# Attention orders on VectorE, key blocks turned two at a time, and the seam from a Mamba layer to a 2:4-sparse feed-forward

## What is computed

```
x = x + attention(layernorm(x))     # 16 heads of 128, clip, ALiBi, causal
x = x + ternary_ffn(layernorm(x))   # bf16, weights quantised by groups of 64
x = x + mamba(layernorm(x))         # 512 channels, 16 states, conv of 4
x = x + sparse_ffn(layernorm(x))    # h = silu(x Wg) * (x Wu), keep the 2 largest of each 4
```

```
scores = clip(q k^T / sqrt(128), -1024, 1024) + slope[h] * j, -inf where j > i
z = softmax(scores) v ;  out = z Wo
h_t = exp(delta_t A) h_(t-1) + delta_t B_t u_t ;  y_t = C_t h_t + D u_t ;  out = (y * silu(z)) Wout
```

## Time and profile before

| | us |
|---|---|
| median of 3 runs (1805.96 to 1808.68) | 1806.5 |
| the profiled execution | 1806.8 |
| its span, first to last instruction | 1804.9 |
| PE busy | 1667.8 (92%) |
| DVE busy | 1414.8 (78%) |
| ACT busy | 1272.2 (70%) |
| POOL busy | 824.5 (46%) |

### The profile page before, as it was taken

One profiled execution on the slowest core, in us unless ns is written; L12 is line 12 of the kernel. 1 busy time (PEld: TensorE's weight loads), 2 busy tenths in 40 slices (PEclk: granted clock), 3 DMA queues, 4 the chain that ended last, 5 costly groups with the idle time before them and its releaser, 6 DMA issues.

```text
span 1804.9 us, 31648 instructions
## 1 busy us (share of the span) xinstructions
PE 1667.8 (92%) x9536; PEld 1363.9 (76%) x9536; DVE 1414.8 (78%) x2299; ACT 1272.2 (70%) x2376; POOL 824.5 (46%) x731
## 2 busy tenths in 40 slices
PE   6899999999999999999997998789799799897998
PEld 4788888888888888888886787566467565456887
DVE  6688777877787777777776666888888788886996
ACT  4677767776777677777774554899895999783442
POOL 3555455545555455545542111059692088780000
PEclk9999999999999999999999999989999999998999
DMA  2000000000000000000001000022220122240000
GB/s 95 19 24 24 23 20 21 23 23 29 9 21 24 26 15 15 26 23 15 15 6 40 10 0 1 4 96 102 82 93 1 50 90 97 70 140 1 1 24 24
DMA packets 25090, 64.14 MB, mean 36 GB/s; under 512 B 2816, under 2 KB 8960, under 8 KB 24768
## 3 DMA queue, kind: packets, MB, share of 16 engines
q1 hardware_dynamic: 25024, 63.31, 10.6%
HBM read 60.94 MB, written 2.36 MB: 35 GB/s over the span
## 4 chain that ended last, share of the span: by engine, by line
PE 54%; POOL 15%; DVE 13%; issue 11%; ACT 5%; DMA 2%; POOLq 0%; DVEq 0%; SPq 0%; ACTq 0%
POOL m_h L2246 12%; PE ps L475 9%; PE ps L548 8%; PE ps L510 8%; PE ps L533 5%; PE ps L488 5%; PE ps L740 4%; PE ps L660 3%; POOL prob L2132 2%; PE ps L752 2%; PE ps L874 2%; PE ps L561 2%; PE ps L681 2%; DVE x L1520 2%; PE ps L908 1%
## 5 line engine op out<-in xcount | busy, mean ns | idle before, releaser
L2246 POOL TENSOR_TENSOR m_h<-m_h,m_C 128x1024 f32<-128x1024 f32 x128 | 305.8, 2392 | 193.9 <-DVE m_h L2024 193.9
L2024 DVE TENSOR_TENSOR_SCAN m_h<-m_y,ps 128x1024 f32<-128x1024 f32 x128 | 291.6, 2284 | 53.4 <-PE ps L867 45.9
L2132 POOL TENSOR_SCALAR prob<-prob 128x896 f32<-128x896 f32 (+7 forms) x256 | 195.8, 765 | 298.8 <-ACT prob L995 270.0
L2139 POOL TENSOR_SCALAR prob<-prob,rinv 128x128 f32<-128x128 f32 (+7 forms) x256 | 237.0, 929 | 161.7 <-DVE rinv L1508 152.3
L1481 DVE TENSOR_TENSOR pt_lo<-ps,pt_hi 128x512 fp32r<-128x512 f32 (+2 forms) x320 | 193.9, 606 | 96.0 <-ACT pt_hi L1008 92.3
L874 PE MATMUL ps<-m_h,ident 128*128 128x512 f32 x512 | 249.1, 610 | 10.8 <-POOL m_h L2246 10.8
L1474 DVE CUSTOM_DVE_ANT_0 prob<-prob,bias 128x640 f32<-128x640 f32 (+7 forms) x256 | 216.5, 859 | 46.8 <-POOL prob L2132 31.4
L1001 ACT ACTIVATE prob<-prob,nmax 128x128 f32<-128x128 f32 (+7 forms) x256 | 197.2, 773 | 43.6 <-DVE nmax L1474 43.6
L1008 ACT ACTIVATE pt_hi<-ps 128x512 fp32r<-128x512 f32 (+2 forms) x320 | 170.3, 532 | 76.3 <-PE ps L533 74.6
L1350 ACT ACTIVATE m_u<-m_uT,m_bT 128x256 f32<-128x256 f32 x512 | 210.6, 494 | 8.6 <-PE ps L867 8.6
L533 PE MATMUL ps<-ident,prob 128*128 128x128 f32 x1152 | 189.8, 274 | 5.5 <-POOL prob L2139 5.4
(11 more groups left out here) (244 smaller groups left out, 4065.1 us busy)
## 6 DMA issues: line engine op xcount, KB each, us to landing
m_C<-bc_dram SPq DMA_DIRECT2D x64, 512.0 KB, 3.6
wqk_raw<-wqk_in SPq DMA_DIRECT2D x16, 512.0 KB, 3.2
wv_raw<-wv_in SPq DMA_DIRECT2D x16, 256.0 KB, 2.6
wo_raw<-wo_in SPq DMA_DIRECT2D x16, 256.0 KB, 2.7
x<-x_in SPq DMA_DIRECT2D x2, 1024.0 KB, 6.7
q_raw<-wgu_in SPq DMA_DIRECT2D x8, 256.0 KB, 2.8
raw<-wgu_in SPq DMA_DIRECT2D x1, 2048.0 KB, 8.2
out<-x SPq DMA_DIRECT2D x8, 256.0 KB, 2.2
```

What stands on the lines that cost most here:

```text
L2024: nc.vector.tensor_tensor_scan(m_h[:, 2 * (v % 2) + e, :], m_da[:, 2 * (v % 2) + e, :], drive(e), 0.0, ALU.mult, ALU.add).then_inc(scan_do ...
L2132: nc.gpsimd.tensor_scalar(prob[:, at:at + n], prob[:, at:at + n], CLIP, -CLIP, ALU.min, ALU.max).then_inc(s_clipped, 1)
L2139: nc.gpsimd.tensor_scalar(prob[:, at:at + n], prob[:, at:at + n], rinv[:, k:k + 1], 1.0, ALU.mult, ALU.mult).then_inc(norm_done, 1)
L2246: nc.gpsimd.tensor_tensor(state, state, m_C[:, v, :], ALU.mult).then_inc(hc_done, 1)
```

## The change

**PE in attention.** At an even position the turns of that key block and of the next are issued together; at an odd one none.

**DVE in attention.** The split of the q/k weights moves from POOL to DVE, for the next pair, in the place of `head_bias(p + 1, nb, 0)`, which moves behind `pt_rest(p, 14)`. The quantisation is cut in five: sums ahead of mask 13, scales behind `recip(p, 12)`, signs ahead of mask 14, values as before, the result behind `pt_rest(p, 16)`. The residual of `out0` goes ahead of the next pair's mask 7. POOL loses `split_qk` altogether.

**Seam.** The barrier is gone. The output projection of batch 1 has PSUM banks of its own (4 to 7); its first half of the channels runs row tiles 0 to 3 and 4 to 7 behind the two last state additions. The first quad's statistics are taken inside the scan of batch 1. DVE ends Mamba in a function of its own, with the sparse norm, its rest and the splits between; the two splits of down and the residual additions go into or ahead of the sparse layer's first unit. ACT interleaves the weight chunks with y. PE turns the sparse rows before the last two quarters of the output projection, and waits for four splits, not six, before the first product.

```diff
                 for pos, name in enumerate(USES):
-                    pe_transposes(pe, p, pos)
+                    if pos % 2 == 0:
+                        pe_transposes(pe, p, pos)
+                        pe_transposes(pe, p, pos + 1)
                     if has(name, begin, last):
                         pe_free(pe, p, pos, begin, last)
                         use(p, b, nb, pos)
...
+        def pe_sparse_turn(pe, q):
+            pe.wait_ge(g_xl_s, 2 * q)
+            for t in range(QUAD):
+                pe.wait_ge(g_xn_s, QUAD * q + t + 1)
+                for k in range(KD):
+                    mm = nc.tensor.transpose(turned_rows(q, k)[:, t * P:(t + 1) * P], g_xn[:, t, k * P:(k + 1) * P],
+                                             ident[:, :])
+                    if t == QUAD - 1:
+                        mm.then_inc(g_xt, 1)
...
-            xt(0)
-            pe.wait_ge(fw_lo, 6)
+            pe.wait_ge(y_skip, 2 * DT)
+            pe.wait_ge(fw_lo, 4)
             for u in range(UNITS - 1):
                 for e in range(4):
                     gate_up(u, e)
+                    if u == 2 and e == 0:
+                        pe.wait_ge(fw_lo, 6)
                     if u >= 2:
                         down(u - 2, e)
+                    if u == 1 and e == 1:
+                        pe.wait_ge(m_o_added, TILES)
                     if u % 2 and e == 1:
-                        xt(u // 2 + 1)
+                        pe_sparse_turn(pe, u // 2 + 1)
...
             for e in range(2):
                 add_state(1, last, RING - 1, e, end=True)
-
-        def pe_mamba_out(pe, b, ks):
+                if b == B - 1:
+                    pe.wait_ge(scan_done, 4 + 2 * B * HALF_UNITS)
+                    pe_mamba_out(pe, b, (0, 1), range(4 * e, 4 * e + 4))
+
+        def pe_mamba_out(pe, b, ks, tiles=range(TILES)):
+
             for k in ks:
                 pe.wait_ge(y_lo, DT * b + k + 1)
-            for t in range(TILES):
+            for t in tiles:
                 seq = [(a, w, k) for k in ks for a, w in passes()]
                 for i, (a, w, k) in enumerate(seq):
-                    mm = nc.tensor.matmul(ps[:, t // 2, (t % 2) * D:(t % 2 + 1) * D],
+                    mm = nc.tensor.matmul(ps[:, 4 * b + t // 2, (t % 2) * D:(t % 2 + 1) * D],
...
-            pe.wait_ge(y_skip, 2 * DT)
-            pe_mamba_out(pe, 1, (0, 1))
+            pe.wait_ge(y_skip, 2 * DT - 1)
+            pe_sparse_turn(pe, 0)
             pe_mamba_out(pe, 1, (2,))
             pe_mamba_out(pe, 1, (3,))
-            phase_end(pe, "pe", PH_M)
...
-            act_ffn_weights(act)
-            act_y_hi(act, 1, 1)
-            phase_end(act, "act", PH_M)
+            act.wait_ge(fw_in, 80)
+            act.wait_ge(da_done, 2 * B * HALF_UNITS)
+            act_ffn_weights(act, (0, 1))
+            act_y_hi(act, 1, (2,))
+            act_ffn_weights(act, (2,))
+            act_y_hi(act, 1, (3,))
+            act_ffn_weights(act, (3,))
+            act_sparse_rows_hi(act, 0)
+            act.wait_ge(scan_done, 4 + 2 * B * HALF_UNITS)
+            act_ffn_weights(act, (4, 5))
...
+            def qk_weights_rest(p):
+                flat = "p a b c -> p (a b c)"
+                dve.wait_ge(w_hi_s, p * 2 + 1)
+                nc.vector.tensor_tensor(wqk_lo[:, :, :, :].rearrange(flat), wqk_raw[:, :, :, :].rearrange(flat),
+                                        wqk_hi[:, :, :, :].bitcast(F32).rearrange(flat),
+                                        ALU.subtract).then_inc(w_lo_s, 1)
...
                 q_start(p, b)
                 if not begin:
                     z_rest(p - 1, 1, 1)
-                if not last:
-                    head_bias(p + 1, nb, 0)
+                if one_on:
+                    qk_weights_rest(p + 1)
                 v_rest(p, 1, USES.index("v1"))
                 pt_rest(p, 2)
                 mask(p, 12)
                 pt_rest(p, 3)
+                q_sums()
                 mask(p, 13)
-                q_scales()
                 if not begin:
                     residual(p - 1, before, 1, USES.index("out1"))
                 pt_rest(p, 4)
                 recip(p, 12)
+                q_scales()
...
+                q_signs()
                 mask(p, 14)
-                q_signs()
...
                 pt_rest(p, 14)
+                if not last:
+                    head_bias(p + 1, nb, 0)
                 z_rest(p, 0, 1)
                 recip(p, 15)
                 pt_rest(p, 15)
                 q_values()
                 next_qk(3)
                 pt_rest(p, 16)
+                q_result()
...
+                residual(p, b, 0, USES.index("out0"))
                 next_mask(7)
-                residual(p, b, 0, USES.index("out0"))
...
             dve_norm_xn(dve, 0, 0, a_xn)
+            qk_weights_rest(0)
             dve_norm_lo(dve, 0, a_xl[0], a_xh[0])
...
-            norm_stats(0)
-            norm(0)
-            xt_lo(0)
             for u in range(UNITS - 1):
...
                 hidden(u, 0)
                 if u:
                     masks()
+                else:
+                    dve_ffn_weights(dve, [4])
                 if u % 2 == 0 and ahead is not None:
-                    norm_stats(ahead)
+                    dve_sparse_stats(dve, ahead)
                 hidden(u, 1)
+                if u == 0:
+                    dve_ffn_weights(dve, [5])
...
                 dve_mamba_y_lo(dve, b, e)
+            if b == B - 1:
+                dve_sparse_stats(dve, 0)
...
+        def dve_mamba_end(dve):
+
+            b = B - 1
+            for e in range(2, DT):
+                dve.wait_ge(y_added, 8 + 2 * HALF_UNITS * (b + 1) - DT + 1 + e)
+                dve_mamba_skip(dve, b, e)
+                dve_mamba_gate(dve, b, e)
+                if e == 2:
+                    dve_ffn_weights(dve, [0])
+            dve_sparse_norm(dve, 0)
+            for e in range(2, DT):
+                dve_mamba_y_lo(dve, b, e)
+            dve.wait_ge(y_lo, B * DT)
+            dve_sparse_rows_lo(dve, 0)
+            dve_ffn_weights(dve, [1, 2, 3])
...
             dve_mamba_post(dve, 1)
-            dve_ffn_weights(dve, range(2, 6))
             dve_mamba_residual(dve, 1)
-            phase_end(dve, "dve", PH_M)
             dve_sparse(dve)
...
-                if two_on:
-                    split_qk(p + 2)
 
             pool_norm(pool, 0)
-            split_qk(0)
...
-            split_qk(1)
-            with pool.Fori(0, LAST_PAIR - 1) as it:
+            with pool.Fori(0, LAST_PAIR) as it:
                 body(it)
-            body(LAST_PAIR - 1, two_on=False)
-            body(LAST_PAIR, two_on=False, last=True)
+            body(LAST_PAIR, last=True)
```

More of the change, by code:

```diff
@@ L296, in drive @@
             return ps[:, 4 + 2 * e:6 + 2 * e, :].rearrange("p a n -> p (a n)")
-        PH_A, PH_F0, PH_M = range(1, 4)
+        PH_A, PH_F0 = range(1, 3)
         STEPS = 8
@@ L1205, in act_ffn, with act_sparse_rows_hi @@
             ht_hi(n_bodies - 1, 1)
+        def act_sparse_rows_hi(act, q):
+            for k in range(KD):
+                act.wait_ge(g_xt, 2 * q + k + 1)
+                nc.scalar.activation(g_xh[:, q % 2, k, :], turned_rows(q, k), ACT.Copy).then_inc(g_xh_s, 1)
         def act_sparse(act):
-            def xt_hi(q):
-                for k in range(KD):
-                    act.wait_ge(g_xt, 2 * q + k + 1)
-                    nc.scalar.activation(g_xh[:, q % 2, k, :], ps[:, 4 + k, :], ACT.Copy).then_inc(g_xh_s, 1)
             def silu(u, e, part=0):
@@ L1383, in act_mamba_scan, with act_y_hi @@
             four(1, last)
-        def act_y_hi(act, b, half):
-            for e in (2 * half, 2 * half + 1):
+        def act_y_hi(act, b, tiles):
+            for e in tiles:
                 act.wait_ge(yz_done, DT * b + e + 1)
@@ L1570, in values, with result @@
                     did(nc.vector.tensor_tensor(q_pos[:, 0:n], q_pos[:, 0:n], q_bf[:, 0:n], ALU.subtract))
+                def result():
                     after()
@@ L1573, in values, with body @@
                     did(nc.vector.tensor_tensor(q_out[:, bass.ds(at, n)], q_bf[:, 0:n], q_pos[:, 0:n], ALU.add))
-                return scales, signs, values
-            def body(p, b, nb, begin=False, before=None):
+                return sums, scales, signs, values, result
+            def body(p, b, nb, begin=False, before=None, one_on=True):
                 last = nb is None
                 before = b if before is None else before
-                q_scales, q_signs, q_values = q_parts(p, b)
+                q_sums, q_scales, q_signs, q_values, q_result = q_parts(p, b)
                 def next_mask(k):
@@ L1715, in dve_attention @@
                 body(it, 1, 1)
-            body(LAST_PAIR, 1, None)
+            body(LAST_PAIR, 1, None, one_on=False)
             z_rest(LAST_PAIR, 1, 1)
@@ L1723, in dve_mamba_residual @@
```

(8 more changed lines are left out.)

77 lines of the change are left out of this document (30 added, 47 removed).

## The result

| | before | changed |
|---|---|---|
| median, us | 1807.2 (6 runs) | 1815.3 (6 runs, 1814.1 to 1817.2) |
| ratio, 95% interval | | 1.0044 (1.0031 to 1.0056) |
| span of the profiled run, us | 1804.9 | 1814.4 |

The change made the kernel slower by 8 us where 11 us less was forecast, and the time is outside the range. The spans of the two profiled runs differ by 9.5 us, and the traces put them in three places. The ternary layer's first product starts at 994.3 before and at 1011.4 after: attention lost 17.0. The last scan instruction of DVE starts at 1618.74 and at 1640.72, 22.0 later: the Mamba stage lost another 4.9. The first gate and up product starts at 1653.57 and at 1662.89, and the span ends 9.5 later: the seam gave 12.5.

The account below looks back on a forecast made before the run. PE was taken to set attention's pace, and the DVE chain the seam's. From the profiled 1806.8 us, +2.4 for attention, -2.3 for the start and -10.7 for the seam gave 1796.2, range 1786 to 1806.

Parts of the forecast that it names:

- A: PE in attention: paired turns cost nothing themselves, but odd blocks' turns wait for `pt_rest`; +0.6 us a body, +0.9 at most.
- The others nothing: Attention: key blocks other than 7, 11 and 15 were to have no wait at their turns.
- B: DVE's orders in attention: in batch 0 -0.2 -0.5 +0.2 us a body; with the pairs +2.4 over sixteen bodies.
- the statistics: Scan of batch 1: the first quad's statistics, where PE already waits 1.4 us, cost +1.8 (ends 0 and +3).
- the swap: Attention: residual ahead of mask 7 moves the wait from `v1` to `out1`; net 0 (ends -1.0 and +0.4).
- C: Kernel start: first projection 1.5 us earlier, first body -0.8 without POOL's split; -2.3 (ends -4 and -0.5).
- D: Seam behind the Mamba scan: -14.2 +1.8 +1.7 = -10.7 us (ends -15 and -5).
- Gate and up and its clock fall: Seam: the product starts at 1641.1 against 1655.25, -14.2 us; a clock fall after PE's pause costs +1.7.
- Rival 1: Attention: DVE's orders help more than counted, 1 us a body, -8 on the sum, 1788.2 us; chance 0.15.
- Rival 2: Attention: the pair waits add up through ACT and DVE, 0.5 us more a body, 1804.2 us; chance 0.15.
- Rival 3: Attention: POOL holds DVE's q/k split in each body, +1 us for 15 bodies, 1811.2 us; chance 0.07.
- Rival 4: Seam gives half, through a further clock fall, stretched DVE work beside POOL or new bank waits; 1801.5 us; chance 0.11.

Follow-up runs that it names:

- e1: The changed kernel with the turns of key blocks one at a time again, all else as changed: 1790.7 us, ratio 0.9908.
- e2: The kernel before with the paired turns alone put in: 1830.4 us, ratio 1.0130.
- e11: As e5, but the residual of `out0` is behind the next pair's mask 7 again, as before the change: 1782.6 us, ratio 0.9856.
- e13: The kernel before with the quantisation cut in five pieces as in the change, and nothing else: 1795.9 us, ratio 0.9928.
- e12: The kernel before with the q/k split alone moved from POOL to DVE, and the first head bias behind `pt_rest(14)`: 1812.4 us, ratio 1.0023.
- e7: As e5, but the split of the q/k weights is POOL's again, all other DVE orders staying: 1821.6 us, ratio 1.0070.
- e3: The changed kernel with the first quad's statistics behind the scan of batch 1, not inside it: 1808.7 us, ratio 1.0010.
- e5: The changed kernel with turns one at a time and the statistics behind the scan: 1784.9 us, ratio 0.9867.

## Why the prediction was wrong, point by point

**A, the pairs: the step that failed.** The place and mechanism were right: the second turn waits for `pt_rest` of two blocks before. At blocks 7, 11 and 15 the predicted 0.2, 0.2 and 0.49 were measured as 0.22, 0.21 and 0.52. Three things were wrong. "The others nothing" left out blocks 13 (0.53 in batch 0) and 19 (0.33 and 0.44), which I hadn't counted through as I had 15. The 0.9 was cut to 0.6 for a lag of PE that no row showed. And in batch 1 half of the 0.6 was let go for the slack of DVE, which covered nothing: there the pairs took 1.87 a body, in batch 0 1.57 (e1). The term was thus +7.2 for the sixteen bodies, and the runs gave +24.6 (e1) and +23 (e2). With 24.6 in its place the sum would be 1796.2 - 7.2 + 24.6 = 1813.6. The other misses below nearly cancel (B was 5 us too careful, the start and the statistics some 5 too hopeful), which is luck.

**B, DVE's orders: half of the gain, and for other reasons.** Without the pairs, the prediction has -0.5 a body in batch 0 and -0.1 in batch 1, -4.8; the runs gave -10.1. That the swap is worth nothing held (e11), and so did its reason: the wait came back before `out1`. The quantisation's pieces were worth more than thought (e13: -13.0), since they clear the wait before the ninth scores as well, which I had put down to the swap, and take 0.5 a body in batch 1 too. The split alone cost 4.6 (e12). What I didn't see is that split and swap hang together (e7).

**C, the start: failed.** DVE's rows came earlier, as thought (PE's first turn starts at 12.62 in place of 14.37), and the first projection did start 1.4 earlier, at 18.31 in place of 19.70, but its first nine products then started 0.43 apart rather than 0.23, which takes 1.8 back. The clock column can't be used here: it reads 1.00 for both stretches, but the trace of the changed kernel has no clock record of its own before 22.2 us, so the durations are what shows it. In both kernels PE was at the slower pace before the projection (its turns stand 0.21 apart, against 0.11 in the earlier trace rows); in the kernel before it came out of a pause of 1.41 us at full pace, in the changed one out of a pause of 1.78 still at the slower one. That the longer pause is the cause isn't shown. The first `q_start` came 0.3 later than before; from trace to trace of kernels with this start it moves between 51.6 and 54.3 us, so that no more can be said than that no clear gain came.

**D, the seam: right, but for the statistics.** Gate and up and its clock fall: -12.5 predicted, -12.7 measured from the end of the scan. (By its own rows the last accumulation ends at 1627.8, not 1627.6, a slip that changes little.) The fall came and cost 1.5 where 1.7 was priced, but it needn't have: behind the same pause there was none in e3 and e5. The statistics cost not 1.8 but 4.8 in the scan, 1.8 of their own and 3.0 with the fall of the clock that the longer wait brought, and 6.5 by e3, where the fall at the seam is gone too. The place I gave them, behind a wait of PE of 1.4, was the warning, and I took it for slack.

**The rivals.** Rival 1 did not come; 1 us a body would also have been 16 on the sum and not 8. Rival 2 (the pair waits add up) named the cause, and stopped at 0.5 a body on top of the 0.6 where the pairs took 1.6 to 1.9. Rival 3's time, 1811.2, lies near the measured one for another reason: DVE's split was held by POOL, but by 0.2 to 0.3 us a body and not 1 (1.43 to 1.52 in the changed kernel for 1.22), and it is the split on POOL that shows the lock in full (e7). Rival 4's further clock fall came in the scan, not at the seam.
